# Four-layer network on one core: set-up of the stages moved into the stages before them, and the values' bias added on VectorE

## The reference, cut to what matters

```python
x = L0_attn_x
xn = _layernorm(x, axis=-1)
x = x + _L0_attn_ref(xn, w_qkv, b_qkv, w_out, b_out) + _L0_ffn_ref(xn, w_gate, w_up, w_down)
xn = _layernorm(x, axis=-1)
x = x + _L1_attn_ref(xn, slope_rate, qkvu_w, qkvu_b, out_w, out_b, theta) + _L1_ffn_ref(xn, w_gate, w_up, w_down)
xn = _layernorm(x, axis=-1)
x = x + _L2_attn_ref(xn, Wq, Wk, Wv, Wo, pek, pev) + _L2_ffn_ref(xn, wqkv, ..., b2)
xn = _layernorm(x, axis=-1)
x = x + _L3_attn_ref(xn, wq, bq, wu, bu) + _L3_ffn_ref(xn, router_w, w1, w2)
```

```python
def fp4_quant_dequant(x):
    scale = jnp.maximum(jnp.max(jnp.abs(xb), axis=-1, keepdims=True) / 6.0, 1e-12)
    idx = jnp.searchsorted(_MID, jnp.abs(xb / scale))
    return (_GRID[idx] * jnp.sign(xb / scale) * scale).reshape(shape)
gate, y = fp4_linear(x, w_gate), fp4_linear(x, w_up)
return fp4_linear(jax.nn.silu(gate) * y, w_down)
```

## Time and profile before

| | us |
|---|---|
| median of 3 runs | 4258.23 (4253.19 to 4263.59) |
| profiled execution: its own time | 4260.68 |
| profiled execution: span of the trace | 4258.7 |
| TensorE busy | 2931.0 (69%) |
| VectorE busy | 2349.2 (55%) |
| ScalarE busy | 1746.5 (41%) |
| GpSimd busy | 826.7 (19%) |
| mean granted TensorE clock | 0.783 of full |

### The profile page before, as it was taken

The page is one execution under the profiler, slowest core; times in us unless marked ns, Lnnn a source line. Parts: engine busy times, 40 slices in busy tenths (PEclk is TensorE's granted clock), DMA queues, the critical chain, the costliest instruction groups (busy, mean ns, idle before and its releaser), DMA issues. The chain is left out here.

```text
span 4258.7 us, 67695 instructions
## 1 busy us (share of the span) xinstructions
PE 2931.0 (69%) x21547; PEld 1596.1 (37%) x21547; DVE 2349.2 (55%) x4792; ACT 1746.5 (41%) x4244; POOL 826.7 (19%) x1061
## 2 busy tenths in 40 slices
PE   5588846374635787777776687777778722768885
PEld 2344424253423444444443343333333311762221
DVE  4556467454855566666663354444445453138885
ACT  2355511211213455455553244444444401227775
POOL 2100001021113444444441300000000004112220
PEclk9789867686767999999998666666666655889998
DMA  3432110000001000000000577777777615663331
GB/s 113 79 56 52 38 53 0 8 1 6 1 14 48 10 19 18 18 10 18 18 18 3 170 189 196 187 192 192 187 193 192 161 42 158 174 146 55 66 61 37
DMA packets 462309, 340.77 MB, mean 80 GB/s; under 512 B 64351, under 2 KB 424986, under 8 KB 461986
## 3 DMA queue, kind: packets, MB, share of 16 engines
q1 hardware_dynamic: 441474, 308.78, 29.4%
q0 software_dynamic: 8704, 20.99, 1.8%
q10 hardware_dynamic: 11808, 7.08, 0.6%
HBM read 174.71 MB, written 146.81 MB: 75 GB/s over the span
## 5 line engine op out<-in xcount | busy, mean ns | idle before, releaser
L1158 DVE TENSOR_REDUCE a_soft_NM<-a_soft_s_ps 128x2 f32<-128x1024 f32 (+3 forms) x512 | 514.2, 1021 | 204.3 <-PE a_soft_s_ps L1093 132.8
L1192 ACT ACTIVATE a_soft_PTS<-a_soft_st_ps 128x512 f32<-128x512 f32 (+3 forms) x1024 | 458.3, 521 | 147.9 <-PE a_soft_st_ps L1069 101.7
L465 PE MATMUL a_soft_pt_ps<-net_ident,a_soft_PR 128*128 128x128 f32 x1280 | 330.1, 370 | 123.2 <-ACT a_soft_PTS L567 115.8
L613 ACT ACTIVATE a_soft_PR<-a_soft_s_ps,a_soft_least 128x128 f32<-128x128 f32 (+3 forms) x512 | 263.9, 527 | 338.7 <-DVE a_soft_least L588 241.8
L1064 PE MATMUL a_soft_st_ps<-a_soft_QS,a_soft_KS 50*128 50x512 bf16 (+4 forms) x1024 | 257.8, 359 | 60.1 <-ACT a_soft_PTS L1192 32.2
L465 PEld LDWEIGHTS a_soft_pt_ps<-net_ident,a_soft_PR 128*128 128x128 f32 x1280 | 184.1, 181 | 220.8 <-ACT a_soft_PR L613 160.0
L1106 PE MATMUL a_soft_o_ps<-a_soft_PTS,a_soft_VR 128*32 128x512 f32 (+3 forms) x2048 | 240.9, 544 | 0.1
L2275 PE MATMUL f_run_ps<-f_run_WQKV,f_run_HT 128*128 128x512 f32 x384 | 228.9, 687 | 15.2 <-DVE f_run_RS L1496 8.0
L2608 ACT ACTIVATE f_run_PB<-f_run_ps,f_run_MX 128x128 f32<-128x128 f32 x512 | 180.3, 378 | 134.0 <-DVE f_run_MX L2490 134.0
L2413 POOL TENSOR_TENSOR f_run_QK<-f_run_QK,f_run_T 128x512 f32<-128x512 f32 x128 | 163.4, 1277 | 365.6 <-DVE f_run_T L2468 363.2
L569 DVE COPY a_soft_PTS<-a_soft_pt_ps 128x512 f32<-128x512 f32 (+3 forms) x320 | 169.5, 530 | 72.6 <-PE a_soft_pt_ps L465 40.0
(11 more groups left out here) (382 smaller groups left out, 6395.5 us busy)
## 6 DMA issues: line engine op xcount, KB each, us to landing
a_soft_BIAS<-skew_d SPq DMA_DIRECT2D x256, 191.0 KB, 4.3
band_d<-a_soft_PR SPq DMA_DIRECT2D x256, 191.0 KB, 3.8
skew_d<-a_soft_RS SPq DMA_DIRECT2D x128, 256.0 KB, 4.5
a_soft_PB<-band_d SPq DMA_DIRECT2D x128, 256.0 KB, 3.1
f_run_W<-in_L_ffn_w SPq DMA_DIRECT2D x72, 256.0 KB, 2.7
query_rows_d<-a_proj_PARTS SPq DMA_DIRECT2D x96, 128.0 KB, 3.4
key_rows_d<-a_proj_PARTS SPq DMA_DIRECT2D x96, 128.0 KB, 3.8
a_soft_QS<-query_rows_d SPq DMA_DIRECT2D x32, 384.0 KB
```

What stands on the lines that cost most here:

```text
L465: last = pe.transpose(pt_ps[:, slot, kb * P:(kb + 1) * P], PR[:, n % NPR, OFF + kb * P:OFF + (kb + 1) * P], ident[:])
L613: act.activation(PR[:, n % NPR, OFF:OFF + width(j)], s_ps[:, n % 4, 0:width(j)], ACT.Exp, bias=least[:, n:n + 1], scale=-1.0).then_inc(pro ...
L1158: dve.tensor_reduce(NM[:, T % 2, j, p, :], s_ps[:, ring["s", a] % 2, :, 0:width(j)], AX.X, ALU.max, negate=True).then_inc(max_ready, 1)
L1192: act.activation(PTS[:, T % 2, 2 * p + par, kb, q0:S], st_ps[:, e % 3, q0:S], ACT.Exp, scale=scale).then_inc(probs_ready, 1)
```

## The change

Seven edits, all of one kind but the last:

- **Layer norms carry set-up.** `layernorm_stage` takes lists: tiles of the input to load in eight pieces (`n0`, statistics per piece, loop written out), loads on SP, matrices to turn on TensorE with copies on ScalarE, a first program for GpSimd and one for ScalarE. The input's load, `a0`'s loads, casts and turnings go into `n0` (40 loads beside the input); `a3`'s go into `n3`; `a1`'s turnings, sine, exponentials and `a2`'s key table go into `n1`.
- **FP4 weights.** `fp4_weights` is gone. Both layers' weights are loaded in `n0` as three matrices of 384 columns each (zeros fill the pads), rounded inside `a0_soft` by VectorE, one of ten instructions every fourth step from `t = 8`, each behind a drain (60 steps), and turned at the start of `fp4_ffn`: nine transposes, three copies.
- **Angles.** L1's angle tables are made by GpSimd between its products of `f0`, batches 1 to 6 (13 instructions, most of 1024 columns), after SP has loaded L1's tables there.
- **Local tables.** L2's tables and weights are loaded in `f1`, and GpSimd casts and scales them between its products, batches 1 to 7. The 24 products with the norm's shift and the scaling of `W1` are done in `f2_run` at steps 14 and 15.
- **Relative tables.** Their differences are made in `n0`, the turning in `f0`, the split and store in `n1`; the 2 MB of bias rows are written in `f0`. `a2` keeps one stage of set-up with six loads.
- **Position bias.** The four rows come from SBUF, not from DRAM.
- **Values.** In the projections of `a0` and `a2` the one-row products and ScalarE's copy go; VectorE adds a bias tile held in all partitions while it copies from PSUM.

```diff
-def layernorm_stage(nc, stage, X, XN, XNT, ident):
+def layernorm_stage(nc, stage, X, XN, XNT, ident, fill=(), loads=(), turns=(), first_pool=None, first_act=None):
...
+        @block.sync
+        def _(sp):
+            for b, src in enumerate(fill):
+                sp.dma_start(X[:, TB * b:TB * (b + 1), :], src).then_inc(x_loaded[b], 16)
+            for dst, src in loads:
+                sp.dma_start(dst, src).then_inc(loaded, 16)
...
+            for b in range(len(fill)):
+                dve.wait_ge(x_loaded[b], 16)
+                for t in range(TB * b, TB * (b + 1)):
+                    dve.bn_stats(st[:, t, :], X[:, t, :])
...
         @block.scalar
+            if first_act is not None:
+                first_act(act)
+            for k, (dst, src) in enumerate(turns):
+                a, b = src.shape
+                act.wait_ge(w_turned, k + 1)
+                act.activation(dst, w_ps[0:b, k % 2, 0:a], ACT.Copy).then_inc(w_copied, 1)
             act.wait_ge(var_ready, 1)
...
         @block.gpsimd
+            if first_pool is not None:
+                if loads:
+                    pool.wait_ge(loaded, 16 * len(loads))
+                first_pool(pool, stored)
             pool.sem_inc(xn_copied, 1)
...
         @block.tensor
+            if loads and turns:
+                pe.wait_ge(loaded, 16 * len(loads))
+            for k, (dst, src) in enumerate(turns):
...
             pe.sem_inc(xt_ready, 1)
...
-                        pe.matmul(out, XNT[:, b * S + j * P:b * S + (j + 1) * P], values[0], start=True, stop=False)
-                        last = pe.matmul(out, values[2], values[1], start=False, stop=True)
+                        last = pe.matmul(v_ps[:, b % 2, j * P:(j + 1) * P], XNT[:, b * S + j * P:b * S + (j + 1) * P], values[0],
+                                         start=True, stop=True)
...
-                if values is not None:
-                    act.wait_ge(v_ready, b + 1)
-                    act.activation(values[3][:, 4 * b:4 * b + 4, :, :].rearrange("p a h (j d) -> p (a h) j d", d=HD),
-                                   v_ps[:, b % 2, :].rearrange("p (j h d) -> p h j d", j=TB, d=HD), ACT.Copy).then_inc(v_copied, 1)
...
+                if values is not None and i % NJ == NJ - 1:
+                    b = i // NJ
+                    dve.wait_ge(v_ready, b + 1)
+                    shift = bass.AP(values[1].tensor, values[1].offset, [list(values[1].ap[0]), [HD, H], [0, TB], [1, HD]])
+                    dve.tensor_tensor(values[2][:, 4 * b:4 * b + 4, :, :].rearrange("p a h (j d) -> p (a h) j d", d=HD),
+                                      v_ps[:, b % 2, :].rearrange("p (j h d) -> p h j d", j=TB, d=HD), shift, ALU.add).then_inc(v_copied, 1)
...
+                if matrices and t >= 8 and t % 4 == 0 and (t - 8) // 4 < FP4_STEPS * len(matrices):
+                    dve.drain()
+                    fp4_step(dve, (t - 8) // 4 % FP4_STEPS, matrices[(t - 8) // 4 // FP4_STEPS], QSC[:], QINV[:], QT[:], QM[:])
...
-def fp4_ffn(nc, stage, X, XN, ident, WGU, WD, clear=None):
+def fp4_ffn(nc, stage, X, XN, ident, RAW, loads, between, clear=None, skew=None, turn=None):
...
             for b in range(B):
+                if b == 1:
+                    pool.wait_ge(loaded, 16 * len(loads))
+                if b >= 1:
+                    between(pool, b)
                 pool.wait_ge(h_rounded, b + 1)
...
+    def angles(self, pool, b):
+        ang, kk, quarter = self.t["ang"], self.t["kk"], self.t["quarter"]
+        if b == 1:
+            for g in range(2):
+                pool.tensor_scalar(ang[:, g, :], self.t["tok_idx"][:], self.t["th"][:, g:g + 1], None, ALU.mult)
+            pool.drain()
+            pool.tensor_scalar(kk[:], ang[:], float(1 / (2 * np.pi)), quarter[:, 0:1], ALU.mult, ALU.add)
...
+        elif b <= 5:
+            step = self.t["TRIG"]
+            pool.tensor_scalar(step[:], kk[:], -TWO_PI[b - 3], None, ALU.mult)
+            pool.drain()
+            pool.tensor_tensor(ang[:], step[:], ang[:], ALU.add)
...
+            def shift(t):
+                out = take(1, t + 1, "shift", 0)
+                for n in range(2):
+                    for i in range(2):
+                        for k, (c0, r) in enumerate(LCHUNKS):
+                            last = pe.matmul(out[0:r, 6 * n + 3 * i + k:6 * n + 3 * i + k + 1], W1[...], GB[:, n, 1:2],
+                                             start=True, stop=True)
...
+                if t == SHIFT:
+                    shift(t)
...
+        transpose_weights(nc, "a2_turn", ident, [(i[n], W[:, k, :]) for k, n in enumerate(("Wq", "Wk", "Wv", "Wo"))],
+                          [(skew_base[:], cst["skew_base"]), (shift[:].rearrange("p (h d) -> p h d", d=HD), bass.AP(pev.tensor, pev.offset, [[0, P], [0, H], [1, HD]]))])
```

More of the change, by code:

```diff
@@ L147, in layernorm_stage @@
         pt = s.ps("pt", [P, 2, TB * P])
+        w_ps = s.ps("w_ps", [P, 2, TB * P])
         var_ready, sd_ready = s.sem("var_ready"), s.sem("sd_ready")
@@ L236, in split_parts, with transpose_weights @@
     return dve.tensor_copy(parts[2], rest)
-def transpose_weights(nc, stage, ident, jobs):
+def transpose_weights(nc, stage, ident, jobs, loads):
     n = len(jobs)
     with Scope(nc, stage) as s:
-        ring = s.sb("ring", [P, 2, P])
-        pt = s.ps("pt", [P, 2, 512])
-        loaded = [s.sem("loaded0"), s.sem("loaded1")]
-        turned, copied = s.sem("turned"), s.sem("copied")
+        ring = s.sb("ring", [P, n, P])
+        pt = s.ps("pt", [P, n, 512])
+        loaded, more_loaded = [s.sem(f"loaded{i}") for i in range(n)], s.sem("more_loaded")
+        turned = s.sem("turned")
         block = s.block()
@@ L1419, in down @@
                 last.then_inc(y_ready, 1)
+            for n in range(3):
+                out = ht_ps[:, n, :] if n < 2 else y_ps[:]
+                for c in range(3):
+                    last = pe.transpose(out[:, c * P:(c + 1) * P], RAW[:, n, c * P:(c + 1) * P], ident[:])
+                last.then_inc(w_turned, 1)
+            if turn is not None:
+                rows, r = turn[1], turn[1].shape[1]
+                pe.wait_ge(w_copied, 1)
+                pe.transpose(ht_ps[0:r, 0, 0:P], rows, ident[:]).then_inc(w_turned, 1)
             turn_x(0)
+            pe.wait_ge(w_copied, 3 if turn is None else 4)
             gate_up(0, 0)
@@ L2646, in token_tiles, with causal_attention @@
     return a.rearrange("b (j p) f -> p (b j) f", p=P)
-def fp4_layer(nc, stage, X, XN, ident, i, clear=None):
-    with Scope(nc, stage) as s:
-        WGU, WD = s.sb("WGU", [P, 2 * FF]), s.sb("WD", [P, 3, P])
-        fp4_weights(nc, f"{stage}_weights", ident, i["w_gate"], i["w_up"], i["w_down"], WGU, WD)
-        fp4_ffn(nc, f"{stage}_run", X, XN, ident, WGU, WD, clear)
-def causal_attention(nc, X, XNT, ident, cst, scratch, i):
+def causal_attention(nc, X, XN, XNT, ident, cst, scratch, i, x_tiles, loads, clear_pads, matrices):
```

567 lines of the change are left out of this document (276 added, 291 removed).

## The result

| | before | after |
|---|---|---|
| median, us | 4257.82 (4253.19 to 4263.59, 4 runs) | 4092.49 (4090.42 to 4100.24, 4 runs) |
| ratio | | 0.9614, 95% interval 0.9597 to 0.9632 |
| profiled execution, span | 4260.68, 4258.7 | 4090.42, 4088.5 |
| TensorE / VectorE / GpSimd busy | 2931.0 / 2349.2 / 826.7 | 2876.8 / 2340.1 / 874.9 |
| mean granted TensorE clock | 0.783 | 0.795 |

The forecast was 4091, between 4066 and 4118. The span fell by 170.2 us where the sum said 167.1. The first view is again the timeline at the edges of the stages; each row is the first or last instruction of one (start, duration, engine, line), except the second, the first write to the ring; `SPq` is an issue of a DMA.

The account below looks back on a forecast made before the run. TensorE bounds `a0_soft` and `f2_run`, VectorE `f0_run`, no engine the set-up between barriers. Gains and costs sum to 167.1 us off the 4258.7 span: 4091.6, median about 4091, range 4066 to 4118.

Parts of the forecast that it names:

- `a2`'s set-up: Between `f2_run` and `a2`'s projection: one stage of six loads stays of 29.7 us; +18.5 us, range +16 to +22.
- `a2_proj`: Projection of `a2`: removing the one-row products gains +5 us, between +2 and +15.
- `f1`: Second fp4 layer: set-up removed, +31.5 us, and GpSimd's added work in `f1_run`, -5.5 us, between -2 and -9.
- Six of the seven stretches of set-up: Set-up moved under other work: `n0` +15.4, fp4 +31.5 twice, `a1` +40.7, `f2` +34.8, `a3` +10.7 us.
- the fp4 weights in both layers: Set-up before `f0_run` and `f1_run`: 32.66 us less one barrier goes, +31.5 us twice.
- the list of loads had taken the statistics' place: In `n0`: the loads become the latest before the first ring write, at 31; with `a0`'s set-up +15.4 us, +12 to +17.
- `a3`: Set-up of `a3`, 3503.47 to 3516.00, 12.5 us less a barrier and 0.7 for late casts: +10.7 us.
- the second of the two that were weighed: `a2_proj`: the same bytes must still be stored, 39 us at 295 GB/s, so the most gained is about +15.
- Contention: GpSimd's added instructions hold up VectorE: -13 us in `f0_run` (18 us times 0.72), -5.5 in `f1_run`.
- `a0_soft`: VectorE's 60 added rounding instructions, about 28 us, mostly absorbed by gaps: -3 us, bounds 0 and -15; position bias 0.
- Moved work setting the end of its new stage: Rival: late moved work in `n0` (4 us), `n1` (2), `a2`'s bias tile (4), `f1` (4); 4105 us, chance 0.10.
- that rival: GpSimd slow: one-input instructions near 4.3 ns a column, up to -35 us in `f0_run`, -9 in `f1_run`; 4116 us, chance 0.12.

Follow-up runs that it names:

- Experiment 3: Changed kernel, but in `n0` TensorE waits only for the first three loads and GpSimd's casts and clears follow its copies to `XN`; 4092.89 us, ratio 0.9581.
- experiment 5: Changed kernel with the 60 rounding steps in `a0_soft` left out, both fp4 layers' weights unrounded; 4149.41 us, one run.

## Why the prediction was right

The total was right by 1.5 us in the median, and nine of the twelve terms by 2.3 us or less, but not all for their reasons. That it is so near is luck: the 13.7 us that `a2`'s set-up fell short are balanced by 6.4 too many in `a2_proj`, 5.3 in `f1` and 3.6 in stages that were put at nothing.

*Set-up.* Six of the seven stretches of set-up moved as worked out: 15.2, 41.2, 35.0 and 10.7 us, and the fp4 weights in both layers. The reason was the one given: nothing there was bound by an engine, and the barrier at each end had put it on the path. Experiment 3 shows the order of `n0` too: the list of loads had taken the statistics' place, landed at 25.8 by the prediction's sum and at 25.36 in the trace. For `a3` the sum is right by a slip: it takes `n3`'s end from GpSimd's copy at 3503.47, while ScalarE's last copy ended at 3504.59; from there the same sum gives 9.6.

*`a2`'s set-up* was the step that failed, by 13.7 us. The prediction named the 2048 pieces and gave the landing "2.7 to 8"; it took 20.7. The upper bound had no row under it, and by the prediction's own terms a landing of 8 would have left some 14 us, not the 16 of its range. No load of the trace of before had so many small pieces, but one could have priced them: the 128 pieces of 32 bytes of `a1`'s `a_run_sl` start within 1.2 us there, 9.1 ns each, which for 2048 is 18.7 us. The terms of issue and turning were right or too high (6.8 where 11.2 stood).

*`a2_proj`* gave 11.4 where 5 was taken, inside its 2 to 15. The mechanism is the second of the two that were weighed, the stores as the new bound. But most of the gain goes with the clock of 0.71 in the trace of before: with the values undone the stage was granted 0.88 in both traces, and the edit was worth 1.2 to 1.5. Equal code was granted 0.79 and 0.93 in `a0_proj`; whether the 0.71 is such a draw, or comes from the set-up stages that stood in front of it, is open. These two errors, -13.7 and +6.4, are both the values' edit, and half cancelled.

*Contention.* 13 was predicted for `f0_run`; it is 15.3 between the two traces (31.5 less the 16.2 of the table), and 14.3 and 11.2 against the kernel without angles. Two errors cancelled: GpSimd's instructions took 29.9 us, not 18 (the multiplications 2.7 ns a column, midway between the 1.3 taken and the small row of 4.3), and a microsecond of them cost VectorE 0.45, not 0.72. In `f1_run` the same step was 5.5 and is 0.6: VectorE's busy time rose by 1.7 us only (137.03 to 138.72), for 8.3 us more of GpSimd's. GpSimd's additions are 1.2 us a batch there and 5 in `f0_run`. So busy share times length is too coarse a price; that the length per batch against the gap in the batch decides is a guess from these two stages.

*`a0_soft`* cost 1.0, not 3, and experiment 5 finds nothing that the rounding costs, within some 2 us. The position bias from SBUF cost nothing: from the stage's first issue to its first product are 31.5 us, 31.4 before.

*The rivals.* Moved work setting the end of its new stage was right in one place, `a2`'s tile, and at over three times its price (13.7 us for 4). GpSimd's 29.9 us lie midway between the 18 of the sum and the 45 of that rival, without its effect. No heavy stage lost clock: 0.91 in `a0_soft` against 0.90, and 0.91 in `f2_run` both times.

## What to carry to other kernels

Set-up between barriers is worth its whole length when it moves under work, and it can be read off two rows; what must be priced with care is what the move brings with it. Look for the pace of a load's pieces in the trace and multiply it by their number, and broadcast over heads in the operand, not in the transfer. As far as the two stages here tell, price contention by the length of one engine's instructions against the other's gap in one round of the loop. Price a stage whose bound engine depends on the granted clock by both clocks, since equal code was granted 0.79 in one trace and 0.93 in another. Where an engine stands still with nothing released, see whether a loop jumps there.
